# Summing exponentials in pairs on VectorE before the ones-matmul, in the last attention stage of a gated attention block

## The chip, the cores and the metric

One core of a Trainium2 chip runs the whole kernel. The metric is the device time of one execution in microseconds (us), median of three runs. TensorE (PE in the views) does matrix products, VectorE (DVE) and ScalarE (ACT) elementwise work, GpSimd (POOL) elementwise work beside them, SyncE (SP) issues the DMAs.

## What is computed

For each of 8 batches of 512 rows by 512 columns, a cross attention with 16 heads of 32 columns, then a quantised feed-forward layer, both added to the input with a gate:

```python
qk = jnp.einsum('bhqd,bhkd->bhqk', Q, K)
scores = qk / math.sqrt(dk)
# a first softmax gives statistics; a tiny MLP makes one temperature t per head of them
t = jnp.exp(log_t)[..., None]
attn_scores = qk / (2.0 * t)
attn = jax.nn.softmax(attn_scores, axis=-1)
out = jnp.einsum('bhqk,bhkd->bhqd', attn, V)
...
x = x + jnp.tanh(g_xattn[0]) * _L0_xattn_ref(_layernorm(x, axis=-1), ctx_1024, ctx_1024, ...)
x = x + jnp.tanh(g_ffn[0]) * _L0_ffn_ref(_layernorm(x, axis=-1), L0_ffn_w1, L0_ffn_w2)
```

So a score matrix is exponentiated twice: once for the statistics ("first softmax", stage A), once with the temperature ("second softmax", stage B). The change is in stage B of the last batch.

## The kernel before

**Rounds.** A software pipeline of ten rounds, i = -1 to 8. Round i does the projections of batch i+1, stage A of batch i, and stage B with everything behind it of batch i-1. So round 8 has only stage B of batch 7, its output projection, its feed-forward layer and the stores: no stage A and no projections. Each engine has its own instruction list, written out by hand in the order of its work; engines meet only at counting semaphores.

**Stage B.** The 16 heads are taken in four groups G of four heads. For each group the 512 keys are taken in four tiles k of 128. One "set" s = 4G + k (0 to 15) is one key tile of the four heads of a group, that is four score tiles g = 0 to 3 of 128 keys x 512 queries. For each score tile:

- `score_b` (L1519): TensorE makes the tile in one of two PSUM buffers `b_ps`, tile g in buffer g % 2. Before it, it waits until ScalarE has exponentiated the tile two before it, which was in the same buffer.
- `second_exp` (L837): ScalarE writes exp(scale x score) in 32 bits to `probs`, which is the SBUF buffer `region1`, two sets deep. For its first tile of a set it waits until the set that used that half before was consumed (`set_used`).

For each set:

- `values` (L1525): four float32 products (32 output rows each, one per head, side by side in TensorE's columns), exponentials times V, into PSUM `o_ps`, summed over the four key tiles of the group. It waits for all four exponentials of the set.
- `denominators` (L1540): four float32 products of the same shape with a matrix of ones, into PSUM `z_ps`: the sums of the exponentials over the keys. Their end is counted in `set_used`.

TensorE's order in the loop over s is: score tiles 0 and 1 of set s, `values` of set s-1, score tiles 2 and 3 of set s, `denominators` of set s-1. After set 15 come its `values` and `denominators`, and then the output projection (L1596 in round 8).

**Once per group** VectorE normalises (`normalise` L1072) in three parts: part 0 copies `o_ps` out (L1080), during set 4(G+1); part 1 waits for the last `denominators` of the group, transposes `z_ps` (L1083) and makes reciprocals (L1085 to L1087), as the first thing in set 4(G+1)+1; part 2 transposes the reciprocals back (L1090) between tiles 1 and 2 of that set. GpSimd then runs `split_y` (L614): a product (L616), a cast (L618), a subtraction (L620), which give the two float16 halves of y for the output projection. Behind group 0's `split_y`, GpSimd's list has `add_bias` (L576): four additions of a 128x512 tile of the residual and a bias row (L581). All of these GpSimd instructions read and write SBUF. VectorE has no other work in round 8 until the output projection.

`qst` and `kst` hold queries and keys in float16, one of two copies for each batch's parity. Batch 7 uses copy 1; copy 0 was last read in round 7.

The other rounds run the same stage B with the score tiles of stage A put between (`set_tiles`); there VectorE has a maximum and a statistic to do for each of those tiles.

Of the kernel before, what the change touches and what calls it, by code (L numbers as in the profile page):

```python
# [19 lines left out]
F32 = mybir.dt.float32  # L20
F16 = mybir.dt.float16
F8 = mybir.dt.float8e4
ALU = mybir.AluOpType
ACT = mybir.ActivationFunctionType
# [4 lines left out]
H, DK = 16, 32  # L29
HID = 2048  # L30
DH = 64
T = S // P
# [3 lines left out]
G4 = P // DK  # L36
# [8 lines left out]
OFFSET = 1536.0  # L45

SETS = C * T


A_PLAN = (40, (2, 2, 2, 2, 1, 1, 1, 1, 1, 1, 1, 1, 2, 2, 2, 2))  # L50
# [90 lines left out]
def nth(b, per, k):  # L141


    return (b + 1) * per + k
# [23 lines left out]
def stages(i):  # L168

    return 0 <= i < B, 1 <= i <= B, i + 1 < B  # L170


def flamingo_kernel(nc, x, ctxT, g_xattn, g_ffn, WqT, bq, WkT, bk, WvT, bv, WoT, bo,
                    w1T, b1, w2T, b2, w3T, b3, f1T, f2T, out):
    with ExitStack() as ctx:
        def sb(name, shape, dt=F32):
            return ctx.enter_context(nc.sbuf_tensor(name, shape, dt))

        def sem(name):
            return ctx.enter_context(nc.semaphore(name))  # L180
# [4 lines left out]
        qst = [sb(f"qst{p}", [P, H, S], F16) for p in range(2)]  # L185
        kst = [sb(f"kst{p}", [P, H, S], F16) for p in range(2)]
# [6 lines left out]

        region1 = sb("region1", [P, 2, T * S])
        probs = region1[:, :, :].rearrange("p s (g q) -> p s g q", g=G4)
        stage_q = region1[:, 0, :].bitcast(F16).rearrange("p (l g n) -> p l g n", l=2, g=C)
        xin = region1[:, 1, :].rearrange("p (t n) -> p t n", t=T)
        xq = region1[:, 1, :].rearrange("p (t n) -> p t n", t=T)
# [34 lines left out]
        ones32 = sb("ones32", [P, P])  # L233
# [49 lines left out]
        def bank(name):  # L283
            return ctx.enter_context(nc.psum_tensor(name, [P, S], F32))

        a_ps = [bank(f"a_ps{n}") for n in range(A_BANKS)]
        b_ps = [bank(f"b_ps{n}") for n in range(2)]
        o_ps, z_ps = bank("o_ps"), bank("z_ps")
# [27 lines left out]
        def per_batch(name, events):  # L316
            s = sem(name)
            per[name] = (s, events)
            return s
# [6 lines left out]
        b_full = per_batch("b_full", H * T)  # L326
        b_exp = per_batch("b_exp", H * T)
        set_used = per_batch("set_used", SETS)
        o_full = per_batch("o_full", C)
        o_out = per_batch("o_out", C)  # L330
        z_out = per_batch("z_out", C)
# [28 lines left out]
        inv2t_done = per_batch("inv2t_done", 1)  # L360
        f_link = per_batch("f_link", LINKS_F)
        hq_done = per_batch("hq_done", T)

        def slot_of(n):
            return (n % G4) * C + n // G4
# [10 lines left out]
        def set_tiles(i, s):  # L376

            sets = a_plan(i)[0]
            if stages(i)[1]:
                if s == 0:  # L380
                    return {}
                first, end = (EARLY + (sets - EARLY) * n // (SETS - 1) for n in (s - 1, s))
            else:
                first, end = (sets * n // SETS for n in (s, s + 1))
            count = end - first
            return {g: first + n for n, g in enumerate({1: (1,), 2: (0, 2), 3: (0, 1, 2)}[count])}
# [390 lines left out]
        def _(act):  # L777
# [59 lines left out]
            def second_exp(b, s, g):  # L837
                slot = slot_of(G4 * (s // T) + g)
                act.wait_ge(b_full, nth(b, H * T, G4 * s + g + 1))
                if s == 0 and g == 0:  # L840
                    act.wait_ge(inv2t_done, nth(b, 1, 1))
                if g == 0:
                    act.wait_ge(set_used, nth(b, SETS, s - 1))
                nc.scalar.activation(probs[:, (s + 1) % 2, g, :], b_ps[g % 2][:, :], ACT.Exp,  # L844
                                     scale=inv2t[:, slot:slot + 1]).then_inc(b_exp, 1)

            def body(i, par):
                has_a, has_b, has_p = stages(i)
                for s in range(SETS):
                    for g in range(G4):  # L850
# [169 lines left out]
        def _(dve):  # L1020
            vec = nc.vector
# [44 lines left out]
            def tile_a(b, k):  # L1066

                row_max(b, k)
                if k >= S_LATE:
                    row_stat(b, k - S_LATE)  # L1070

            def normalise(b, G, part):  # L1072

                c = Chain(dve, norm_link, LINKS_NORM, b)
                c.n = 3 * G
                z_own = zrow.rearrange("p (j c) -> p j c", c=DK)[:, :, 0]
                if part == 0:
                    dve.wait_ge(o_full, nth(b, C, G + 1))
                    dve.wait_ge(y_done, nth(b, C, G))
                    vec.tensor_scalar(y32, o_ps[:, :], LOWEST, None, ALU.max).then_inc(o_out, 1)  # L1080
                elif part == 1:
                    dve.wait_ge(set_used, nth(b, SETS, T * (G + 1)))
                    vec.transpose(zrow, z_ps[:, :]).then_inc(z_out, 1)  # L1083
                    dve.wait_ge(z_out, nth(b, C, G + 1))
                    c.link(vec.tensor_scalar(zwide[:, :], z_own, 1e-30, None, ALU.max))  # L1085
                    c.link(vec.reciprocal(zwide[:, :], zwide[:, :]))
                    c.link(vec.scalar_tensor_tensor(out=zinv[:, :], in0=z_own, scalar=0.0, in1=zwide[:, :],  # L1087
                                                    op0=ALU.is_ge, op1=ALU.mult))
                else:
                    vec.transpose(zrow, zinv[:, :].unsqueeze(2).broadcast_to([P, S // DK, DK])) \  # L1090
                        .then_inc(zrow_done, 1)

            def features(b, par):

# [113 lines left out]
            def stat_x(b, pair):  # L1208
                tiles = (2 * pair, 2 * pair + 1)
                for n in tiles:  # L1210
                    dve.wait_ge(x_in[n % 2], b * 32 + 16 * (pair + 1) - 32)
                for n in tiles:
                    ins = vec.bn_stats(st6[:, X_ORDER[n], :], cin[:, n % 2, :])
                ins.then_inc(p_link, 1)
                dve.wait_ge(p_link, nth(b, 2, pair + 1))
                for n in tiles:
                    ins = vec.bn_aggr(mv1[:, X_ORDER[n], :], st6[:, X_ORDER[n], :])
                ins.then_inc(mv1_done, 1)
# [71 lines left out]
            def ternary_sum(k):  # L1290
                dve.wait_ge(f_abs, 1 + max(MAGNITUDE_ORDER.index(n) for n in range(4 * k, 4 * k + 4)))
                vec.tensor_reduce(wsum[:, k:k + 1], wabs[:, k, :], AX.X, ALU.add).then_inc(f_sum, 1)
# [53 lines left out]
            def body(i, par):  # L1346
                has_a, has_b, has_p = stages(i)
                second = i == 0
                for s in range(SETS):
                    for g in range(G4):  # L1350
                        if has_a and g in set_tiles(i, s):
                            tile_a(i, set_tiles(i, s)[g])
                        if has_b and (s % T, g) in NORM_AT and s >= T:
                            normalise(i - 1, s // T - 1, NORM_AT.index((s % T, g)))
                    if has_p and has_b and s in X_STATS_AT:
                        stat_x(i + 1, X_STATS_AT.index(s))
                    if second and s == BIAS_AT:
                        join_biases()
                    if second and s in SUMS_AT:
                        ternary_sum(SUMS_AT[s])  # L1360
                    if second and s in SCALES_AT:
                        ternary_scale(SCALES_AT[s])
                    if second and s in TERNARY_AT:
                        make_ternary(TERNARY_AT[s])
# [5 lines left out]
                if has_b:  # L1370
                    normalise(i - 1, C - 1, 0)
                    normalise(i - 1, C - 1, 1)
# [31 lines left out]
                if has_b and has_p:  # L1404
                    c.link(residual_stat(i, T - 1))
                    for t in range(T):
                        ins = vec.bn_aggr(mv2[:, t, :], st6[:, t, :])
# [59 lines left out]
        def _(pe):  # L1467
            mat = nc.tensor.matmul
# [56 lines left out]
            def values(i, has_p, b, par, s):  # L1525

                G, k = s // T, s % T
                pe.wait_ge(b_exp, nth(b, H * T, G4 * (s + 1)))
                if k == 0 and G > 0:
                    pe.wait_ge(o_out, nth(b, C, G))  # L1530
                if s == 0:
                    rested(i, has_p, [o_ps, z_ps])
                for g in range(G4):
                    n = G4 * G + g
                    ins = mat(o_ps[g * DK:(g + 1) * DK, :], vbuf[par][:, k, n * DK:(n + 1) * DK],  # L1535
                              probs[:, (s + 1) % 2, g, :], start=k == 0, stop=k == T - 1)
                if k == T - 1:
                    ins.then_inc(o_full, 1)

            def denominators(b, s):  # L1540

                G, k = s // T, s % T
                if k == 0 and G > 0:
                    pe.wait_ge(z_out, nth(b, C, G))
                for g in range(G4):
                    ins = mat(z_ps[g * DK:(g + 1) * DK, :], ones32[:, 0:DK], probs[:, (s + 1) % 2, g, :],  # L1546
                              start=k == 0, stop=k == T - 1)
                ins.then_inc(set_used, 1)

            def body(i, par):  # L1550
# [283 lines left out]
```

## Time and profile before

| | |
|---|---|
| median of 3 runs | 1297.36 us (1297.17 to 1297.47) |
| the profiled execution | 1297.59 us |
| its span, first to last instruction | 1295.8 us |
| mean granted TensorE clock | 0.970 of full |
| TensorE busy | 1167.2 us (90% of the span) |
| VectorE busy | 1072.5 us (83%) |
| ScalarE busy | 945.0 us (73%) |
| GpSimd busy | 463.5 us (36%) |

Busy shares are of the whole span. Stage B of batch 7 is the stretch from about 1191 to 1239 us of it. Rows of the trace give a start and a duration; "x2" or "x8" is a run of so many instructions in one row, and its duration is that of the run. A matmul row of the float32 products counts two instructions for each of the four tiles, so "x8" is one `values` or one `denominators`. A duration of TensorE contains the time for its result to come out, so that back-to-back instructions overlap: starts, not durations, show its pace.

### The profile page before, as it was taken

Reading aid. Unit: us, or ns where it says so; the run is one execution under the profiler, and the core shown is the slowest. Engines: PE = TensorE matmul, PEld = TensorE weight load, DVE = VectorE, ACT = ScalarE, POOL = GpSimd, SP = SyncE. Lnnn points to the kernel's source line nnn. Section 1 sums busy time; section 2 is a strip of 40 time slices with the busy share of each in tenths; the row PEclk is TensorE's granted clock in tenths of the full one; section 3 lists DMA queues with packets and bytes.
Section 4 is the critical chain, followed back from the end, with each engine's and each line's share of the span. In section 5 each row is a group of like instructions: output and inputs, shape, how many; then the busy total and the mean of one; then the engine's idle time right before and its main releaser. Section 6 shows DMA issues by size and latency. Waiting matters only on the chain.

```text
span 1295.8 us, 19185 instructions
## 1 busy us (share of the span) xinstructions
PE 1167.2 (90%) x6644; PEld 435.0 (34%) x6644; DVE 1072.5 (83%) x1968; ACT 945.0 (73%) x1593; POOL 463.5 (36%) x523
## 2 busy tenths in 40 slices
PE   4867589999999999999999999999999999969978
PEld 2322211444124432344224431344224431224224
DVE  6699779897898889887998879897898879984256
ACT  4588689676985779675985779765985769775833
POOL 3138566520553226530463226511463203120320
PEclk9969789999999999999999999999999999979989
DMA  8822130211202230102202221012202220001000
GB/s 301 233 80 66 37 95 17 50 43 56 66 17 50 58 104 20 42 22 61 90 18 49 50 74 58 21 29 66 98 17 50 50 66 1 1 0 66 1 1 33
DMA packets 36400, 73.09 MB, mean 56 GB/s; under 512 B 8656, under 2 KB 9040, under 8 KB 35792
## 3 DMA queue, kind: packets, MB, share of 16 engines
q1 hardware_dynamic: 36304, 71.87, 19.6%
q8 instruction: 53, 0.87, 0.3%
q14 instruction: 43, 0.35, 0.1%
HBM read 38.13 MB, written 8.39 MB: 36 GB/s over the span
## 4 chain that ended last, share of the span: by engine, by line
PE 50%; DVE 30%; ACT 8%; issue 5%; POOL 1%; SPq 1%; DMA 0%; POOLq 0%; DVEq 0%; ACTq 0%
DVE nmax L1042 8%; DVE stat L1052 6%; PE b_ps L1492 6%; PE b_ps L1522 6%; PE o_ps L1740 6%; PE z_ps L1546 6%; PE o_ps L1535 6%; PE a_ps L1516 4%; PE o_ps L1492 4%; DVE hmax L1254 3%; PE z_ps L1492 2%; PE z_ps L1740 2%; ACT region L844 2%; PE b_ps L1706 2%; ACT etile L812 2%
## 5 line engine op out<-in xcount | busy, mean ns | idle before, releaser
L812 ACT ACTIVATE etile<-a_ps,nmax 128x512 f32<-128x512 f32 x512 | 352.1, 702 | 87.9 <-DVE nmax L1042 86.7
L1042 DVE TENSOR_REDUCE nmax<-a_ps 128x1 f32<-128x512 f32 x512 | 345.4, 679 | 57.5 <-PE a_ps L1516 55.6
L844 ACT ACTIVATE region<-b_ps,inv2t 128x512 f32<-128x512 f32 x512 | 335.0, 704 | 46.8 <-PE b_ps L1522 43.0
L1052 DVE BATCH_NORM_STATS2 stat<-etile 128x6 f32<-128x512 f32 x492 | 335.3, 684 | 10.2 <-ACT etile L812 10.1
L1516 PE MATMUL a_ps<-kst,qst 96*128 96x512 f16 x512 | 196.3, 392 | 31.7 <-ACT etile L812 25.7
L1522 PE MATMUL b_ps<-qst,kst 97*128 97x512 f16 x512 | 193.8, 388 | 11.0 <-ACT region L986 5.6
L1535 PE MATMUL o_ps<-region,vbuf 128*32 128x512 f32 x1024 | 137.2, 607 | 15.0 <-DVE region L1080 8.7
L708 POOL TENSOR_TENSOR region<-region 128x512 f16<-128x512 f32 x64 | 76.6, 1198 | 193.7 <-ACT region L887 193.2
L1546 PE MATMUL z_ps<-region,ones 128*32 128x512 f32 x1024 | 136.4, 604 | 8.1 <-DVE region L1083 8.1
L1522 PEld LDWEIGHTS b_ps<-qst,kst 97*128 97x128 f16 x512 | 49.6, 97 | 251.0 <-ACT region L844 201.9
L616 POOL TENSOR_TENSOR region<-region 128x512 f32<-128x512 f32 x32 | 40.9, 1277 | 245.8 <-DVE region L1090 245.8
L1254 DVE TENSOR_REDUCE hmax<-region 128x1 f32<-128x512 f32 x128 | 81.9, 679 | 17.6 <-ACT region L976 16.0
L586 POOL CAST c_hi<-cin 128x512 f16<-128x512 f32 x28 | 17.1, 611 | 211.3 <-DMA cin<-in_ctxT_dram 211.1
L1516 PEld LDWEIGHTS a_ps<-kst,qst 96*128 96x128 f16 x512 | 51.0, 100 | 86.4 <-ACT etile L812 36.5
L1740 PE MATMUL o_ps<-f,region 128*128 128x512 fp8e4 x352 | 79.6, 379 | 0.0
L1706 PE MATMUL b_ps<-f,region 128*128 128x512 fp8e4 x256 | 63.1, 384 | 5.9 <-DVE region L1280 3.0
L634 POOL TENSOR_SCALAR cin<-cin,mv,rstd 128x512 f32<-128x512 f32 x28 | 58.0, 2081 | 1.5
L976 ACT ACTIVATE region<-b_ps,xmax 128x512 f32<-128x512 f32 x64 | 43.1, 689 | 17.1 <-PE b_ps L1706 16.1
L986 ACT ACTIVATE region<-b_ps 128x1024 f16<-128x1024 f16 x31 | 31.7, 1023 | 30.6 <-PE b_ps L1717 30.5
L1080 DVE TENSOR_SCALAR region<-o_ps 128x512 f32<-128x512 f32 x32 | 21.8, 680 | 36.0 <-PE o_ps L1535 35.8
L1740 PEld LDWEIGHTS o_ps<-f,region 128*128 128x128 f16 x352 | 33.8, 98 | 38.0
L1535 PEld LDWEIGHTS o_ps<-region,vbuf 128*32 128x32 f32 x1024 | 21.0, 108 | 68.2 <-issue 56.9
(325 smaller groups left out, 1997.9 us busy)
## 6 DMA issues: line engine op xcount, KB each, us to landing
kst<-region SPq DMA_DIRECT2D x96, 128.0 KB, 2.3
qst<-region SPq DMA_DIRECT2D x84, 128.0 KB, 2.3
xres<-in_x_dram SPq DMA_DIRECT2D x8, 1024.0 KB, 5.4
out_dram<-xres SPq DMA_DIRECT2D x32, 256.0 KB, 2.0
cin<-in_ctxT_dram SPq DMA_DIRECT2D x30, 256.0 KB, 2.9
cin<-in_x_dram SPq DMA_DIRECT2D x28, 256.0 KB, 2.6
kst<-in_f1T_dram SPq DMA_DIRECT2D x2, 1024.0 KB, 9.8
qst<-in_f2T_dram SPq DMA_DIRECT2D x2, 1024.0 KB, 9.3
```

The costliest lines, as they stand in the source:

```text
L812: nc.scalar.activation(etile[:, k % E_SLOTS, :], a_ps[k % A_BANKS][:, :], ACT.Exp, bias=nmax[:, slot_of(n), t:t + 1], scale=1.0, accum_out ...
L844: nc.scalar.activation(probs[:, (s + 1) % 2, g, :], b_ps[g % 2][:, :], ACT.Exp, scale=inv2t[:, slot:slot + 1]).then_inc(b_exp, 1)
L1042: vec.tensor_reduce(nmax[:, slot_of(k // T), k % T:k % T + 1], a_ps[k % A_BANKS][:, :], AX.X, ALU.max, negate=True).then_inc(a_max, 1)
L1052: vec.bn_stats(stat[:, slot_of(k // T) * T + k % T, :], etile[:, k % E_SLOTS, :]).then_inc(a_stat, covered)
L1254: ins = vec.tensor_reduce(hmax[:, n:n + 1], hbuf[t % 2][:, n * S:(n + 1) * S], AX.X, ALU.max, apply_absolute_value=True)
L1492: ins = mat(mm_ps[bank_n][:, :], left[l](c), right[r](c), start=(c, l, r) == pairs[0], stop=(c, l, r) == pairs[-1])
L1516: mat(a_ps[k % A_BANKS][:, :], qst[par][0:SHIFT, slot, t * P:(t + 1) * P], kst[par][0:SHIFT, slot, :], start=True, stop=True).then_inc(a_f ...
L1522: mat(b_ps[g % 2][:, :], kst[par][0:SHIFT + 1, slot, k * P:(k + 1) * P], qst[par][0:SHIFT + 1, slot, :], start=True, stop=True).then_inc(b ...
L1535: ins = mat(o_ps[g * DK:(g + 1) * DK, :], vbuf[par][:, k, n * DK:(n + 1) * DK], probs[:, (s + 1) % 2, g, :], start=k == 0, stop=k == T - 1)
L1546: ins = mat(z_ps[g * DK:(g + 1) * DK, :], ones32[:, 0:DK], probs[:, (s + 1) % 2, g, :], start=k == 0, stop=k == T - 1)
L1706: ins = mat(mm_ps[bank_n][:, :], xqT[:, c, t * P:(t + 1) * P], f1[:, c, n * S:(n + 1) * S], start=c == 0, stop=c == C - 1)
L1740: ins = mat(mm_ps[bank_n][:, :], hT[t % 2][:, k, :], f2[:, k, :], start=k == 0, stop=k == KC - 1)
```

## The change

In batch 7 alone (`LAST = 7`):

- Two more buffers, each two sets deep, are laid over the free copies: `more_probs` over `kst[0]` for exponentials, `pair_sum` over `qst[0]` for sums. Sets with s % 4 in (0, 1) write to `probs`, those with s % 4 in (2, 3) to `more_probs`.
- `add_pair`: at every odd set s, VectorE adds, tile by tile, the exponentials of set s-1 and set s (float32, 128x512, both from SBUF, the result to SBUF). These 32 additions are in VectorE's list at (s, g), behind the part of `normalise` that stands at that place.
- `denominators` does nothing for even s. For odd s it waits for the four additions and runs its four products on the sums. Eight of the sixteen groups of four products are left.
- ScalarE's wait for a free buffer becomes one wait per two sets, on the pair two before.

```diff
+        more_probs, pair_sum = (a[:, :, :].bitcast(F32).rearrange("p (s g n) q -> p s g (n q)", s=2, g=G4)
+                                for a in (kst[0], qst[0]))
...
+        def exps(b, s):
+            if in_pairs(b) and s % 4 >= 2:
+                return more_probs[:, s % 2, :, :]
+            return probs[:, (s + 1) % 2, :, :]
...
-                if g == 0:
+                if g == 0 and not in_pairs(b):
                     act.wait_ge(set_used, nth(b, SETS, s - 1))
-                nc.scalar.activation(probs[:, (s + 1) % 2, g, :], b_ps[g % 2][:, :], ACT.Exp,
+                elif g == 0 and s % 2 == 0:
+                    act.wait_ge(set_used, nth(b, SETS, max(0, s // 2 - 1)))
+                nc.scalar.activation(exps(b, s)[:, g, :], b_ps[g % 2][:, :], ACT.Exp,
...
-                    dve.wait_ge(set_used, nth(b, SETS, T * (G + 1)))
+                    dve.wait_ge(set_used, nth(b, SETS, T * (G + 1) // (2 if in_pairs(b) else 1)))
...
+            def add_pair(b, s, g):
+
+                j = s // 2
+                dve.wait_ge(b_exp, nth(b, H * T, G4 * s + g + 1))
+                if j >= 2:
+                    dve.wait_ge(set_used, nth(b, SETS, j - 1))
+                vec.tensor_tensor(pair_sum[:, j % 2, g, :], exps(b, s - 1)[:, g, :], exps(b, s)[:, g, :], ALU.add) \
+                    .then_inc(pair_done, 1)
...
+                        if in_pairs(i - 1) and s % 2 == 1:
+                            add_pair(i - 1, s, g)
...
-                              probs[:, (s + 1) % 2, g, :], start=k == 0, stop=k == T - 1)
+                              exps(b, s)[:, g, :], start=k == 0, stop=k == T - 1)
...
                 G, k = s // T, s % T
-                if k == 0 and G > 0:
+                if in_pairs(b) and s % 2 == 0:
+                    return
+                begin = k == (1 if in_pairs(b) else 0)
+                if begin and G > 0:
                     pe.wait_ge(z_out, nth(b, C, G))
+                if in_pairs(b):
+                    pe.wait_ge(pair_done, G4 * (s // 2 + 1))
                 for g in range(G4):
-                    ins = mat(z_ps[g * DK:(g + 1) * DK, :], ones32[:, 0:DK], probs[:, (s + 1) % 2, g, :],
-                              start=k == 0, stop=k == T - 1)
+                    ins = mat(z_ps[g * DK:(g + 1) * DK, :], ones32[:, 0:DK],
+                              pair_sum[:, s // 2 % 2, g, :] if in_pairs(b) else exps(b, s)[:, g, :],
+                              start=begin, stop=k == T - 1)
                 ins.then_inc(set_used, 1)
```

## Rows read from the trace of the kernel before

**Rows 1.** Busy time and clock of a stretch: PE, PEld, DVE, ACT, POOL, PEclk, DMA, GB/s

```profile
1204.00:1216.00 12.00, 12.00 (x81) 2.75 (x80) 2.46 (x7) 10.02 (x16) 8.00 (x7) 1.00 0.01 1
```

**Rows 2.** Chain of work that ended last, inside stage B: start, us, what

```profile
1212.72 0.54 PE b_ps L1522 x2
1213.26 0.99 PE o_ps L1535 x8
```

**Rows 3.** Timeline, a regular half set of stage B

```profile
1194.21 0.60 PE L1522 MATMUL b_ps<-qst,kst 97*128 97x512 f16 x2
1194.64 1.27 ACT L844 ACTIVATE region<-b_ps,inv2t 128x512 f32<-128x512 f32 x2 [0.27 <-PE b_ps L1522]
1194.75 1.06 PE L1535 MATMUL o_ps<-region,vbuf 128*32 128x512 f32 x8
1195.74 0.60 PE L1522 MATMUL b_ps<-qst,kst 97*128 97x512 f16 x2
```

**Rows 4.** Timeline, the half set whose exponentials began late

```profile
1200.82 1.27 ACT L844 ACTIVATE region<-b_ps,inv2t 128x512 f32<-128x512 f32 x2 [0.31 <-PE b_ps L1522]
1201.88 0.65 PE L1522 MATMUL b_ps<-qst,kst 97*128 97x512 f16 x2
1202.14 0.10 PEld L1522 LDWEIGHTS b_ps<-qst,kst 97*128 97x128 f16 x1 [0.17 <-ACT region L844]
```

**Rows 5.** Timeline, the end of stage B

```profile
1236.09 1.27 ACT L844 ACTIVATE region<-b_ps,inv2t 128x512 f32<-128x512 f32 x2 [0.27 <-PE b_ps L1522]
1237.41 1.06 PE L1535 MATMUL o_ps<-region,vbuf 128*32 128x512 f32 x8
1238.29 1.04 PE L1546 MATMUL z_ps<-region,ones 128*32 128x512 f32 x8
```

**Rows 6.** Timeline, set 3's denominators and what follows on VectorE and GpSimd

```profile
1202.46 1.06 PE L1546 MATMUL z_ps<-region,ones 128*32 128x512 f32 x8
1205.06 0.71 DVE L1090 STREAM_TRANSPOSE region<-zinv 128x512 f32<-128x512 f32 x1
1205.42 1.27 ACT L844 ACTIVATE region<-b_ps,inv2t 128x512 f32<-128x512 f32 x2 [0.27 <-PE b_ps L1522]
1205.85 1.28 POOL L616 TENSOR_TENSOR region<-region 128x512 f32<-128x512 f32 x1 [47.69 <-DVE region L1090]
1207.20 0.61 POOL L618 CAST region<-region 128x512 f16<-128x512 f32 x1
1207.89 1.16 POOL L620 TENSOR_TENSOR region<-region 128x512 f16<-128x512 f32 x1
1209.01 4.99 POOL L581 TENSOR_TENSOR xres<-xres,bias_row 128x512 f32<-128x512 f32 x4
1209.59 0.60 PE L1522 MATMUL b_ps<-qst,kst 97*128 97x512 f16 x2
```

**Rows 7.** Timeline, start of the kernel, VectorE and GpSimd alone

```profile
19.49 0.54 DVE L1195 TENSOR_SCALAR region<-region,mv,rstd 128x512 f32<-128x512 f32 x1
19.95 0.68 DVE L1205 TENSOR_TENSOR x_more<-region,x_more 128x512 f16<-128x512 f32 x1
19.97 1.68 POOL L708 TENSOR_TENSOR region<-region 128x512 f16<-128x512 f32 x1 [1.97 <-ACT region L887]
20.55 1.38 DVE L1193 TENSOR_SCALAR region<-region,mv,rstd 128x512 f16<-128x512 f32 x1
24.66 2.25 DVE L1205 TENSOR_TENSOR region<-region 128x512 f16<-128x512 f32 x2
25.09 1.27 POOL L708 TENSOR_TENSOR region<-region 128x512 f16<-128x512 f32 x1 [1.09 <-ACT region L887]
```

**Rows 8.** All instructions of a line: ns min/median/max, first and last start us, form

```profile
L1205 DVE TENSOR_TENSOR region<-region x2: 680/1162/1643, 24.7 to 25.3; 128x512 f16<-128x512 f32 x2
```

**Rows 9.** Stretches of 2 us with TensorE's busy time, granted clock, DMA, GB/s

```profile
1250.00:1252.00 2.00, 0.00 (x0) 1.00 0.00 0
1252.00:1254.00 2.00, 0.00 (x0) 0.80 0.00 0
```

More of the change, by code:

```diff
@@ L47 @@
 SETS = C * T
+LAST = 7
 A_PLAN = (40, (2, 2, 2, 2, 1, 1, 1, 1, 1, 1, 1, 1, 2, 2, 2, 2))
@@ L328, in flamingo_kernel @@
         set_used = per_batch("set_used", SETS)
+        pair_done = sem("pair_done")
         o_full = per_batch("o_full", C)
@@ L362, in flamingo_kernel, with in_pairs @@
         hq_done = per_batch("hq_done", T)
+        def in_pairs(b):
+            return b == LAST
+        def exps(b, s):
+            if in_pairs(b) and s % 4 >= 2:
+                return more_probs[:, s % 2, :, :]
+            return probs[:, (s + 1) % 2, :, :]
         def slot_of(n):
```

## The prediction

> **What bounds the kernel now.** The change touches only stage B of batch 7, so I read that stage alone. First the busy time by stretches: TensorE is busy in all of 12 us, at full clock, ScalarE in 10.0, VectorE in 2.5 and GpSimd in 8.0 [rows 1]. That looks like a stage bound by TensorE. Next the chain of work that ended last: it stays on TensorE here, two score tiles for 0.54 us, four float32 products for 0.99, and again [rows 2]. A half set is thus 1.533 us, a set 3.07, two sets 6.13.
>
> Then the timeline of a half set, to see how near the others are [rows 3]. Score pair at 1194.21; its exponentials start 0.43 later, at 1194.64, and the pair takes 1.27, to 1195.91; the products start at 1194.75; the next score pair at 1195.74. A run of two scores is 0.60 with the second one's own 0.38 in it, so the second score starts about 0.22 behind the first, at 1195.96. That second score has to wait for the second exponential, which ended at 1195.91, 0.05 before. So TensorE is full, but its second score starts at the first moment at which the exponentials allow it. The proof that this is an edge is the one place where the exponentials began late: 0.47 after their scores (1200.35, half a set before 1201.88), they ended at 1202.09, and the second score came at 1202.14, released by ScalarE, instead of 0.22 after 1201.88 [rows 4]. Two loops have the same length here: TensorE's own work, and scores - exponentials - scores through two PSUM buffers.
>
> **The change part by part.**
>
> *The eight groups of ones-products removed.* Each costs TensorE 0.99 us, eight are 8 us, and by busy time alone that would be the gain. What is late next? Take an odd set; its third score starts at time 0, the sums that used to follow its fourth score are gone. Exponentials of tiles 2 and 3: 0.43 to 1.70. Tile 0 of the next set needs the first of them; tile 1 needs the second, so starts at 1.70 + 0.05 = 1.75. The products of `values` start 0.32 behind the second score (1194.75 less 1194.43), at 2.07. With the sums in place it was 0.54 + 0.99 + 0.54 = 2.07. The whole 0.99 becomes a wait for ScalarE's exponentials. From there on the half sets are the old ones: 1.53 each. So seven of the eight removed groups give 0.0 us each, with an uncertainty of about 0.02 each (the 0.43 was 0.47 once), 0.15 together. The eighth is the one of set 14, in set 15: before, `values` of set 15 started at 1237.41, right behind the last exponential (1236.09 + 1.27) [rows 5]; the sums in front were over by then. 0 again. Total gain: 0.0, at most 0.2.
>
> *ScalarE's waits* are on the pair two before, consumed two sets earlier: 0. The exponentials go to another SBUF address: same instruction, 0.
>
> *The 32 additions on VectorE.* The nearest row is a subtraction of two SBUF tiles of that size: 0.68 us alone, the next instruction given 0.60 behind its start [rows 7, 8]. That hides easily in a plain odd set: the exponentials of its tiles end 0.69 or so after they start, the last at 1.70, an addition ends at 2.4, and the sums are wanted on TensorE only behind the second half of the next set, at 0 + 2.07 + 0.99 + 0.54 = 3.60. 1.2 us of cover. At the end, the last addition runs from 1237.4 to about 1238.1, the sums are wanted at 1238.29 [rows 5]: 0, with 0.15 of cover.
>
> *Sets 5, 9 and 13* have `normalise` in front of the additions. Set 3's sums start at 1202.46; VectorE has the reciprocals at 1205.06, where L1090 starts today [rows 6]. Now two additions come first (1205.06, 1205.66), L1090 runs 1206.26 to 1206.97, the third addition starts at 1206.86, the fourth at 1207.46, ending 1208.14. The tiles' exponentials are done by 1206.69, so VectorE is the late one. The sums of set 5 are wanted at 1202.46 + 6.13 = 1208.59. Still 0.4 of cover, if VectorE is not held.
>
> *It will be held, by GpSimd.* L616 starts when L1090 is over, now at about 1207.05: in the middle of the additions. The trace shows what two such instructions do to each other [rows 7]: a VectorE subtraction at 19.95 and a GpSimd subtraction at 19.97; the latter takes 1.68 where L620, of the same form, takes 1.16 [rows 6], so it was held until 20.49, 0.14 before the former's end. VectorE's next instruction, given at 20.55, takes 1.38 instead of 0.54: held until 21.39, 0.26 before GpSimd's end. And of the two subtractions at 24.66, the second took 1.64 instead of 0.68 [rows 8]: held until 26.23, 0.13 before GpSimd's end at 26.36; GpSimd, which had come at 25.09, got in between two VectorE instructions that stood back to back. So: one at a time; whoever waits gets in at the other's next boundary; a VectorE addition holds for 0.54, GpSimd gives back 0.13 to 0.26 before its end, I take 0.20.
>
> Set 5 by these: the third addition holds 1206.86 to 1207.40; L616 runs 1207.40 to 1208.68 and gives back at 1208.48; fourth addition 1208.48 to 1209.16, seen on TensorE 0.05 later, 1209.21. Wanted at 1208.59: 0.62 late. TensorE's list is in order, so the scores of the next set queue behind those sums, and with them the exponentials. Nothing gives this back, because both loops above are full. The same for sets 9 and 13: 3 x 0.62 = 1.9 us.
>
> Set 7 has the bias additions. L618 waits for the fourth addition (holding to 1209.02), 0.61, then L620, 1.16, to 1210.86; the four L581 follow at once, 1.24 apart when alone [rows 6]. Set 7's first scores were at 1209.59, now 1210.21; their exponentials end at 1211.33 and 1211.9, those of tiles 2 and 3 by 1213.5. The first L581 gives back at 1211.90. From there the two engines take turns, 0.54 for an addition and 1.08 for an L581, 1.62 a turn: additions start at 1211.90, 1213.52, 1215.14 and 1216.76, the last ends at 1217.44, seen at 1217.49. Wanted at 1208.59 + 6.13 + 0.62 = 1215.34. 2.15 late. GpSimd is then done; group 1's and group 2's `split_y` end before the next plain set, so sets 11 and 15 are clean.
>
> Sum: 0.0 + 3 x 0.62 + 2.15 = +4.0 us. Bounds: with 0.26 given back, 3 x 0.56 + 1.9 = 3.6; with 0.13, 3 x 0.69 + 2.45 = 4.5; if VectorE cannot get in between the four L581 (no row shows it), its four additions follow at 1215.6 and set 7 is 2.8 late: 4.7. The Trainium skill, page "SBUF — State Buffer", section "SBUF: two separate sides", says that VectorE and GpSimd take turns on a shared pair of ports, each for its full instruction. The trace agrees on the turns, but not on the full duration (given back 0.13 to 0.26 early). By the page the turns would be 0.68 + 1.28, set 5 would be 0.95 late and set 7 3.5: +6.4.
>
> The profiled execution took 1297.59, 0.23 above the median of the runs; 1297.59 + 4.0 - 0.23 = 1301.4.
>
> **The rivals.** 0.2% is 2.6 us here; less than that is no change by this measurement.
> - *Nothing gained, nothing lost* (1297.4, 17%): the additions are hidden after all, because two float32 inputs on VectorE and GpSimd's product do not meet as at 20 us. For it: 0.4 and 1.2 us of cover. Against: rows 7 show the same kinds of instruction. The sums would be released by TensorE's order, not by VectorE.
> - *VectorE keeps its place between back-to-back additions* (1298 to 1299.5, 10%): sets 5, 9 and 13 on time, only set 7 late by up to 2.1. Against: the instruction of 25.09, which got in.
> - *Full turns, as by the page* (1303.8, 8%).
> - *The clock* (1303.4, 9%): in the stall of set 7 TensorE idles some 2 us beside other waits. Elsewhere it idled from 1250 and the clock fell in the second 2 us [rows 9]. If it fell here, about 4 us of work at half clock would add 2. Against: the 2 us before the fall were still at 1.00.
> - *TensorE's time is given back* (1290.4, 6%): seven times 0.99. It needs the second score of a pair at 0.22 behind the first though its buffer's exponential is running. It decides at ScalarE's pair: shorter than 1.27 from score to score. Rows 4 speak against it.
>
> **How the numbers follow.** Forecast as worked out, 50%, with a range of its own from 1300.4 to 1302.3. Slower by over 0.2%: forecast, full turns and clock, 0.67. Within: the first two rivals, 0.27. Faster: 0.06. The range that holds 8 in 10 takes in the first two rivals below and most of the two above: 1297.0 to 1303.5.
>
> **What would show it.** In the profile after: TensorE busy 8 us less; where a group of sums is gone, score pairs 1.2 us and more apart, with waits for L844, and `values` still 2.07 behind the third score; the sums (L1546's successor) waiting for VectorE's additions in sets 5, 7, 9, 13, most in 7; additions of over 1 us beside L616 and L581, and L581 in four rows over 6 us instead of 4.99. The forecast is wrong if additions stay at 0.68 beside GpSimd, or if a score starts before the exponential two before it is over.

## The result, and the profile after

| | before | changed |
|---|---|---|
| median of 6 runs | 1297.36 us | 1302.09 us |
| range | 1296.33 to 1297.58 | 1301.05 to 1302.72 |
| ratio | | 1.0039, 95% interval 1.0028 to 1.0050 |
| profiled execution, span | 1297.59, 1295.8 us | 1301.05, 1299.3 us |
| TensorE, VectorE busy | 1167.2, 1072.5 us | 1162.8, 1098.8 us |

The median became 4.7 us longer, clear of the noise; 4.0 had been forecast. In the changed kernel L1547 makes the scores, L858 the exponentials, L1560 is `values`, L1576 the ones-products, L1113 the additions, L1104 the transpose that ends the normalisation, L628, L630 and L632 `split_y`, L593 the bias additions.

First the places where a group of ones-products is gone. Timeline of the changed kernel, set 5 (start, us, engine, line, what):

```profile
1202.97 0.61 PE L1547 MATMUL b_ps<-qst,kst 97*128 97x512 f16 x2
1204.14 0.39 PE L1547 MATMUL b_ps<-qst,kst 97*128 97x512 f16 x1 [0.57 <-ACT region L858]
1204.71 0.39 PE L1547 MATMUL b_ps<-qst,kst 97*128 97x512 f16 x1 [0.19 <-ACT region L858]
1205.03 1.07 PE L1560 MATMUL o_ps<-region,vbuf 128*32 128x512 f32 x8
```

Where [rows 3] had pairs 1.53 apart with products between them, the next score now comes 1.17 behind the third, its partner 0.57 later, both released by ScalarE, and `values` starts at 2.06: the 2.07 of before. Nothing was gained there.

Then VectorE and GpSimd in the same stretch:

```profile
1203.04 1.29 DVE L1113 TENSOR_TENSOR qst<-region 128x512 f32<-128x512 f32 x2
1204.25 0.70 DVE L1104 STREAM_TRANSPOSE region<-zinv 128x512 f32<-128x512 f32 x1
1204.87 2.33 DVE L1113 TENSOR_TENSOR qst<-region 128x512 f32<-128x512 f32 x2
1205.03 1.63 POOL L628 TENSOR_TENSOR region<-region 128x512 f32<-128x512 f32 x1 [47.30 <-DVE region L1104]
1206.03 0.60 PE L1547 MATMUL b_ps<-qst,kst 97*128 97x512 f16 x2
1207.35 1.06 PE L1576 MATMUL z_ps<-qst,ones 128*32 128x512 f32 x8 [0.71 <-DVE qst L1113]
1208.87 6.30 POOL L593 TENSOR_TENSOR xres<-xres,bias_row 128x512 f32<-128x512 f32 x4
1209.50 6.22 DVE L1113 TENSOR_TENSOR qst<-kst 128x512 f32<-128x512 f32 x4 [2.29 <-ACT kst L858]
1212.95 0.61 PE L1547 MATMUL b_ps<-qst,kst 97*128 97x512 f16 x2
1215.78 1.93 PE L1576 MATMUL z_ps<-qst,ones 128*32 128x512 f32 x8 [2.22 <-DVE qst L1113]
1217.64 1.03 PE L1547 MATMUL b_ps<-qst,kst 97*128 97x512 f16 x2
1217.78 0.72 DVE L1097 STREAM_TRANSPOSE region<-z_ps 128x512 f32<-128x512 f32 x1 [1.46 <-PE z_ps L1576]
1218.60 1.20 PE L1560 MATMUL o_ps<-region,vbuf 128*32 128x512 f32 x8
1219.74 0.60 PE L1547 MATMUL b_ps<-qst,kst 97*128 97x512 f16 x2
1223.57 1.06 PE L1576 MATMUL z_ps<-qst,ones 128*32 128x512 f32 x8 [0.16 <-DVE qst L1113]
```

Two additions alone take 1.29; the two that meet L628 take 2.33, and L628 takes 1.63 instead of the 1.28 of [rows 6]. The four that meet the bias additions take 6.22, and those 6.30 instead of 4.99. The sums of set 5 start at 1207.35; without the wait they would have started 0.53 behind the scores of 1206.03, at 1206.56: 0.79 late. Set 7: 1212.95 + 0.53 = 1213.48, started at 1215.78: 2.30 late. By the same reading sets 5, 7, 9 and 13 are late by 0.79, 2.30, 0.23 and 0.79. (The number in brackets in a row, 0.71 or 2.22, is the idle time that the profile counts; the lateness is 0.07 or 0.08 more.)

The ones-products of set 7 then took 1.93 us instead of 1.06 and the scores behind them 1.03 instead of 0.60. Busy time and clock of that stretch, changed kernel (us, PE, PEld, DVE, ACT, POOL, granted clock, DMA, GB/s):

```profile
1204.00:1216.00 12.00, 7.99 (x48) 1.77 (x52) 9.71 (x9) 8.07 (x14) 9.99 (x7) 0.98 0.00 1
1216.00:1220.00 4.00, 4.00 (x20) 0.45 (x12) 2.41 (x7) 1.27 (x2) 0.00 (x0) 0.63 0.00 0
```

Of these 12 us TensorE was busy in 7.99, against 12.00 [rows 1], and the clock fell to its half level (1.2 GHz) for about 3 us: in stretches of 1 us it is 0.76 from 1215, 0.50 from 1216 and 1217, 0.53 from 1218 and 1.00 from 1219. From the ones-products to the next scores took 1.86 instead of 1.00, from the scores to `values` 0.96 instead of 0.53, from `values` to the scores 1.14 instead of 1.00: 1.4 us in all.

In what follows "the stage" is the time from the first `values` of batch 7 to the first product of the output projection in the profiled execution. It was 47.58 us before (1191.68 to 1239.26) and 53.05 after (1189.70 to 1242.75): +5.5, of which the stalls are 4.1 and the clock 1.4. The rows at its two ends, of the kernel before and then of the changed kernel:

```profile
1191.68 1.07 PE L1535 MATMUL o_ps<-region,vbuf 128*32 128x512 f32 x8 [0.50 <-ACT region L844]
1239.26 0.39 PE L1596 MATMUL b_ps<-wo_hi,region 128*128 128x512 f16 x1
1189.70 1.07 PE L1560 MATMUL o_ps<-region,vbuf 128*32 128x512 f32 x8 [0.50 <-ACT region L858]
1242.75 0.39 PE L1627 MATMUL b_ps<-wo_hi,region 128*128 128x512 f16 x1
```

Behind the stage both kernels take 56.5. The spans differ by 3.5 only, because the code ahead of the stage, the same in both, was 2.0 us shorter in this execution; over the profiles of this study the stage began between 1189.7 and 1193.8. So its length is given below beside the medians of whole runs.

### The profile page after: what moved, and what is told of

It is laid out like the page before. It is cut to its first block, busy times and chain, and to the rows that moved or that the text cites. A ratio compares the mean times of both kernels' runs of the same rounds, so it can differ in the third digit from the quotient of the medians.

```text
span 1299.3 us, 19108 instructions
## 1 busy us (share of the span) xinstructions
PE 1162.8 (89%) x6580; PEld 433.0 (33%) x6580; DVE 1098.8 (85%) x2000; ACT 944.3 (73%) x1593; POOL 466.1 (36%) x523
## 4 chain that ended last, share of the span: by engine, by line
PE 47%; DVE 32%; ACT 8%; issue 6%; POOL 1%; SPq 1%; DMA 0%; POOLq 0%; DVEq 0%; ACTq 0%
DVE nmax L1056 8%; PE b_ps L1517 6%; DVE stat L1066 6%; PE o_ps L1771 6%; PE z_ps L1576 5%; PE b_ps L1547 5%; PE o_ps L1560 5%; PE a_ps L1541 4%; PE o_ps L1517 4%; DVE hmax L1277 3%; PE z_ps L1517 2%; PE z_ps L1771 2%; ACT region L858 2%; PE b_ps L1737 2%; ACT etile L824 2%
## 5 line engine op out<-in xcount | busy, mean ns | idle before, releaser
L858 ACT ACTIVATE region<-b_ps,inv2t 128x512 f32<-128x512 f32 x480 | 314.7, 705 | 46.6 <-PE b_ps L1547 42.7
L1547 PE MATMUL b_ps<-qst,kst 97*128 97x512 f16 x512 | 195.5, 390 | 16.3 <-ACT region L1000 5.6
L1560 PE MATMUL o_ps<-region,vbuf 128*32 128x512 f32 x960 | 128.9, 608 | 14.8 <-DVE region L1094 8.7
L1547 PEld LDWEIGHTS b_ps<-qst,kst 97*128 97x128 f16 x512 | 48.7, 97 | 253.7 <-ACT region L858 190.9
L628 POOL TENSOR_TENSOR region<-region 128x512 f32<-128x512 f32 x32 | 41.8, 1308 | 246.5 <-DVE region L1104 246.5
L1576 PE MATMUL z_ps<-region,ones 128*32 128x512 f32 x896 | 119.4, 605 | 8.1 <-DVE region L1097 8.1
L1517 PE MATMUL b_ps<-region,wq_hi 128*128 128x512 f16 x128 | 41.1, 404 | 3.2 <-ACT region L929 3.2
L636 POOL TENSOR_SCALAR rstd<-mv 128x2 f32<-128x2 f32 (+1 forms) x25 | 5.7, 229 | 105.6 <-DVE mv L1432 44.9
```

Of the source, the lines that this page charges most:

```text
L858: nc.scalar.activation(exps(b, s)[:, g, :], b_ps[g % 2][:, :], ACT.Exp, scale=inv2t[:, slot:slot + 1]).then_inc(b_exp, 1)
L1517: ins = mat(mm_ps[bank_n][:, :], left[l](c), right[r](c), start=(c, l, r) == pairs[0], stop=(c, l, r) == pairs[-1])
L1547: mat(b_ps[g % 2][:, :], kst[par][0:SHIFT + 1, slot, k * P:(k + 1) * P], qst[par][0:SHIFT + 1, slot, :], start=True, stop=True).then_inc(b ...
L1576: ins = mat(z_ps[g * DK:(g + 1) * DK, :], ones32[:, 0:DK], pair_sum[:, s // 2 % 2, g, :] if in_pairs(b) else exps(b, s)[:, g, :], start=be ...
```

## The experiments

Each kernel was timed beside the kernel before, whose median was 1297.17 us beside e1 to e4, 1297.52 beside e5 to e8 and 1297.21 beside e9 to e12. The ratios are to these.

| | median us | ratio | interval | the stage us |
|---|---|---|---|---|
| before | 1297.36 | 1 | | 47.58 |
| changed | 1302.09 | 1.0039 | 1.0028 to 1.0050 | 53.05 |
| e1 half the sums, no additions | 1297.04 | 0.9999 | 0.9990 to 1.0008 | 47.54 |
| e2 bias first | 1302.92 | 1.0042 | 1.0028 to 1.0056 | 52.33 |
| e3 transpose last | 1300.28 | 1.0022 | 1.0013 to 1.0031 | 50.02 |
| e4 both | 1301.70 | 1.0026 | 1.0015 to 1.0037 | 51.88 |
| e5 before, four score buffers | 1296.66 | 0.9992 | 0.9983 to 1.0001 | 47.54 |
| e6 changed, four score buffers | 1302.21 | 1.0035 | 1.0023 to 1.0048 | 52.71 |
| e7 e4 and four buffers | 1296.43 | 0.9989 | 0.9980 to 0.9998 | 46.76 |
| e8 e1 and four buffers | 1294.85 | 0.9977 | 0.9966 to 0.9987 | 45.27 |
| e9 e3, bias gated | 1297.34 | 1.0000 | 0.9991 to 1.0009 | 47.66 |
| e10 e9 and four buffers | 1295.62 | 0.9985 | 0.9976 to 0.9994 | 45.73 |
| e11 e10, products together | 1292.95 | 0.9966 | 0.9952 to 0.9979 | 43.00 |
| e12 before, four buffers, products together | 1292.68 | 0.9961 | 0.9949 to 0.9974 | 43.32 |

### Does the removed work give anything back? (e1)

```diff
-                if in_pairs(b):
-                    pe.wait_ge(pair_done, G4 * (s // 2 + 1))
...
-                              pair_sum[:, s // 2 % 2, g, :] if in_pairs(b) else exps(b, s)[:, g, :],
+                              exps(b, s)[:, g, :],
...
-                        if in_pairs(i - 1) and s % 2 == 1:
-                            add_pair(i - 1, s, g)
```

It also raises batch 7's sums to at least 1e20 instead of 1e-30 ahead of the reciprocal (the clamp, L1099 of the changed kernel); the instruction is the same one with another constant.

> This kernel is the one before with the eight groups of ones-products of the even sets of batch 7 left out and nothing put in their place: no additions on VectorE, no wait for them. It leaves out half of the softmax denominator there (and clamps the rest), so its output is not the reference's. Theory A (the loop scores - exponentials - scores is as long as TensorE's own work): the 8 us of TensorE work turn into waits for ScalarE, time 1297.4 us, within 0.3 of before; two sets stay at 6.13 us. Rival (TensorE is the bound): 7 x 0.99 us come back, 1290.4 us.

Measured: 1297.04 us, ratio 0.9999; the stage 47.54. Timeline of e1, one pair of sets (L1545 scores, L1558 values, L1572 ones-products):

```profile
1210.42 0.60 PE L1545 MATMUL b_ps<-qst,kst 97*128 97x512 f16 x2
1210.85 1.27 ACT L858 ACTIVATE kst<-b_ps,inv2t 128x512 f32<-128x512 f32 x2 [0.27 <-PE b_ps L1545]
1211.59 0.39 PE L1545 MATMUL b_ps<-qst,kst 97*128 97x512 f16 x1 [0.56 <-ACT kst L858]
1212.17 0.39 PE L1545 MATMUL b_ps<-qst,kst 97*128 97x512 f16 x1 [0.19 <-ACT kst L858]
1212.49 1.07 PE L1558 MATMUL o_ps<-kst,vbuf 128*32 128x512 f32 x8
```

Busy times of a stretch of e1:

```profile
1192.00:1204.00 12.00, 10.49 (x68) 2.24 (x64) 1.73 (x4) 9.49 (x16) 0.00 (x0) 1.00 0.30 102
```

Scores at 1210.42, values at 1212.49: 2.07, as with the ones-products between them. TensorE is busy 10.49 of 12 us where it was 12.00, and no faster. So TensorE's work alone is not the bound: without an eighth of its work the stage is as long, and its scores are released by ScalarE. Whether TensorE's own work is shorter than that loop or just as long, e1 can't say; e5 below does.

### Where does the loss come from? (e2, e3, e4, e9)

e2 puts the bias additions ahead of `split_y`, e3 moves the transpose behind the four additions, e4 does both:

```diff
+                if has_b and in_pairs(i - 1):
+                    add_bias(i - 1)
+                    split_y(i - 1, 0)
...
-                        if has_b and (s % T, g) in NORM_AT and s >= T:
+                        if has_b and (s % T, g) in NORM_AT and s >= T and not (in_pairs(i - 1) and (s % T, g) == NORM_AT[2]):
...
                             add_pair(i - 1, s, g)
+                            if (s % T, g) == (1, G4 - 1) and s >= T:
+                                normalise(i - 1, s // T - 1, 2)
```

> The changed kernel with GpSimd's four bias additions (L593 there) ahead of group 0's split_y in round 8. They then run at about 1199 to 1204 us, before set 7's additions, and only meet the first addition of set 5. Theory B (VectorE's additions and GpSimd's SBUF instructions take turns, and TensorE waits for the last addition): set 7's stall of 2.3 us and the clock's fall behind it go, set 5 becomes up to 0.8 us later; 2.4 to 3.2 us above before, 1299.8 to 1300.6 us. Rival (the loss is a cost of the additions or buffers themselves): unchanged, about 1302 us.

Measured: 1302.92 us, the stage +4.75. That is far outside the expected range and near the rival's number, but the profile doesn't show the rival's even cost: the ones-products of three sets wait for VectorE, 1.73 us in set 3 and 0.71 in sets 9 and 13, those of sets 5 and 7 don't, and the clock is at 0.50 for about 3 us behind the first. Why set 3, e4 shows.

> The changed kernel with part 2 of the normalisation (the transpose that releases GpSimd's split_y) behind the fourth addition of sets 5, 9 and 13 instead of between the second and third. Theory B: those additions meet no GpSimd instruction, the three stalls of 0.8 us go; the bias additions still meet set 7, later by about 0.4 us: 2.7 us above before, or 4.1 if the clock falls as in the changed kernel's profile, 1300 to 1301.5 us. Rival (a cost of the additions themselves): unchanged, about 1302 us.

Measured: 1300.28 us, the stage +2.44. The three stalls of sets 5, 9 and 13 are gone, and of the ones-products one group waits for VectorE, that of set 7, with 2.28 us. The clock stayed at 1.00 here.

> The changed kernel with both edits: bias additions first, transpose last. All 32 additions are kept, and so are the eight groups of products on their sums. Theory B: no addition is late for TensorE, 1297.4 us, within 0.5 of before, and by theory A no faster either. Rival 1 (TensorE's removed work comes back once the stalls are gone): 1290 to 1292 us. Rival 2 (a cost of the additions themselves): over 1300 us.

Measured: 1301.70 us, outside what was expected and within the second rival's range. The seven executions spread from 1299.01 to 1302.53, and the profiled one is the longest. Timeline of e4, set 3 (L1116 additions, L1581 ones-products, L1565 values):

```profile
1199.09 5.73 DVE L1116 TENSOR_TENSOR qst<-kst 128x512 f32<-128x512 f32 x4 [3.31 <-ACT kst L861]
1199.46 6.50 POOL L593 TENSOR_TENSOR xres<-xres,bias_row 128x512 f32<-128x512 f32 x4 [40.63 <-DMA xres<-in_x_dram]
1204.87 1.07 PE L1581 MATMUL z_ps<-qst,ones 128*32 128x512 f32 x8 [1.73 <-DVE qst L1116]
1206.46 1.94 PE L1565 MATMUL o_ps<-region,vbuf 128*32 128x512 f32 x8
1213.42 1.06 PE L1581 MATMUL z_ps<-qst,ones 128*32 128x512 f32 x8
```

Busy times of a stretch of e4:

```profile
1208.00:1212.00 4.00, 3.65 (x16) 0.54 (x12) 2.68 (x5) 2.53 (x4) 0.31 (x1) 0.50 0.00 0
```

The bias additions start when the residual's DMA has landed, at 1199.46, and that is 0.37 us into the additions of set 3, which I had taken to be over. The collision was moved, not removed: the ones-products of set 3 wait 1.73 us in e2 and in e4, and in both the clock fell afterwards (granted clock 0.50 in this row). In e4 it stayed down for about 7 us, and set 5's ones-products start 8.55 us behind set 3's (1204.87 to 1213.42) where two sets take 6.13: 2.4 us, which with the 1.8 by which set 3 is late makes 4.2 of the stage's +4.30. e9 puts the bias additions where VectorE is counted to be through:

```diff
+                    pool.wait_ge(pair_done, 2 * G4)
+                    add_bias(i - 1, (0, 1))
+                    split_y(i - 1, 0)
+                    pool.wait_ge(pair_done, 4 * G4)
+                    add_bias(i - 1, (2, 3))
```

> The changed kernel with the transpose last, and GpSimd's four bias additions split so that they fall between VectorE's groups: two once the additions of set 3 are counted, two once those of set 7 are. Bias first had put them on top of set 3's additions. Theory B: no group of additions is late for TensorE, no TensorE wait for VectorE over 0.1 us in the stage, its clock stays full: 1297.4 us, within 0.4 of before, and by theory A not faster. Rival (a loss of the additions that no neighbour explains): over 1299 us.

Measured: 1297.34 us, ratio 1.0000; the stage 47.66, no ones-product waits for VectorE. GpSimd in e9, these at their undisturbed lengths:

```profile
1201.01 2.51 POOL L593 TENSOR_TENSOR xres<-xres,bias_row 128x512 f32<-128x512 f32 x2 [43.17 <-DVE qst L1119]
1207.88 1.28 POOL L628 TENSOR_TENSOR region<-region 128x512 f32<-128x512 f32 x1 [4.36 <-DVE region L1110]
1213.51 2.50 POOL L593 TENSOR_TENSOR xres<-xres,bias_row 128x512 f32<-128x512 f32 x2 [2.43 <-DVE qst L1119]
```

All additions and all products of the changed kernel are there, and the whole loss is gone. It came from the meeting with GpSimd, with the clock's fall behind the stall, and within the interval of 0.1% nothing else was lost or won. One meeting is left and costs nothing: the four additions of set 7 run beside the subtraction of `split_y` and take 3.06 us instead of the 2.50 of set 5's, but still end before TensorE wants the sums.

### What would make the removed work count? (e5 to e8, e10 to e12)

Four score buffers, on the PSUM banks that stage A doesn't use in round 8:

```diff
+        def score_ps(b, s, g):
+            return a_ps[g] if b == 7 and s > 0 else b_ps[g % 2]
...
+                if b == 7 and s == 1 and g == 0:
+                    pe.wait_ge(a_exp, nth(b, H * T, H * T))
+                if b == 7 and s > 0:
+                    pe.wait_ge(b_exp, nth(b, H * T, G4 * s + g - 3))
```

> The kernel before, with the score tiles of sets 1 to 15 of batch 7 in four PSUM buffers (a_ps, free in that round) instead of two; a score waits for the exponential of the tile four before. All ones-products kept. Theory A: TensorE's own work is 6.13 us for two sets with or without the exponentials' wait, so nothing moves: 1297.4 us, within 0.3. Rival (the exponentials' loop is the longer of the two): faster by 1 us or more.

Measured: 1296.66 us, 0.4 below the lower end of what was expected; the ratio is 0.9992 with 1 just inside its interval, and the stage is 47.54 as before. No score has to wait for the exponential two before it any more, and TensorE's own work is 6.13 for two sets too: with e1 this shows two loops of one length.

> The changed kernel with four score buffers. Theory A: the loop through ScalarE is no longer the limit; TensorE's work for two sets is 6.13 - 0.99 - 0.11 = 5.03 us, ScalarE's 8 x 0.585 = 4.7; up to 7.7 us come back, less what the additions are late: they are wanted 1.1 us earlier in every pair, so sets 5, 9 and 13 are late by 1.9 each and set 7 by 3.4 or more, 9 us. Together 1298 to 1301 us, between the two kernels. Rival (buffers do not matter): as the changed kernel, 1302 us.

Measured: 1302.21 us, a little above the expected range; the stage 52.71. Four groups of ones-products wait for VectorE, 0.17 to 2.54 us, and one of them runs for 1.93 us, at the half clock. The number is the rival's, but not its reason: four buffers do give something (e8), and these waits, 4.8 us in all, and the clock cover it. The profiled execution took 1305.42, the longest of the five.

> The changed kernel with four score buffers, bias additions first and the transpose last. Theory A and B together: two sets take about 5.03 us, the additions are late by at most 1 us in sets 5, 9 and 13 in all together 2: 1290 to 1292 us, faster than both kernels. Rival (TensorE's removed work cannot come back because ScalarE or VectorE is the next bound): 1296 to 1298 us.

Measured: 1296.43 us, the stage -0.8: far from the expected 1291 and inside the rival's range. Two groups wait for VectorE, 0.96 us in set 3 and 0.24 in the last; the rest of what is missing is the wait that e8 shows.

> The kernel of half the ones-products and no additions (it leaves out half of the softmax denominator of batch 7 and clamps the rest), with four score buffers. Theory A: with the two-buffer loop gone, the removed products come back: two sets 5.03 us, 1289.7 us (7.7 below before). Rival (another limit, for example the wait of the values' products for all four exponentials): little gain, over 1295 us.

Measured: 1294.85 us, the stage -2.3, not -7.7 as the sum had it; the rival's reason holds. Timeline of e8 (L1553 scores, L1566 values):

```profile
1198.59 1.04 PE L1553 MATMUL a_ps<-qst,kst 97*128 97x512 f16 x4
1199.02 1.26 ACT L861 ACTIVATE kst<-a_ps,inv2t 128x512 f32<-128x512 f32 x2 [0.27 <-PE a_ps L1553]
1200.33 1.07 PE L1566 MATMUL o_ps<-kst,vbuf 128*32 128x512 f32 x8 [0.71 <-ACT kst L861]
```

`values` stands behind the second score of the next set and needs the fourth exponential of its own, which was begun 0.6 us after 1199.02: third score to values is 1.74 instead of 2.07, 7 x 0.33 = 2.3. That wait I had not counted in the sums of e6, e7 and e8, though the rival of e8 names it.

> The same with four score buffers. Half sums with four buffers gave the stage 2.3 us less than before, its profile shows values waiting 0.71 us for the fourth exponential of its set. Additions on time: the same 2.3 us less, 1295.1 us. Rival (additions still late): 1296 to 1297 us.

Measured: 1295.62 us, the stage -1.85: 0.5 above what was expected. One group, the last, waits 0.24 us for VectorE.

For e11 and e12 `values` moves behind the fourth score, in front of the ones-products:

```diff
-                            if s > 0 and g == 1:
+                            if s > 0 and g == (3 if i == 8 else 1):
                                 values(i, has_p, i - 1, 1 - par, s - 1)
```

> The same with values of set s-1 behind the fourth score of set s, next to the sums, instead of behind the second. Then values no longer wait for an exponential that was just begun, and the two kinds of float32 products stand together. TensorE per two sets: 8 scores at 0.215, three groups of products at 0.87, and the changes between them, 4.8 us; ScalarE 8 x 0.585 = 4.7, with some idle at each turn, 5.1. 5 to 7 us below before, 1290.5 to 1292.5 us. Rival (additions are late for sums that are wanted 1.2 us earlier in every pair): 1293 to 1296 us.

Measured: 1292.95 us, the stage -4.6, between the forecast and its rival: four ones-product groups wait for VectorE again, 0.45 to 0.90 us. Timeline of e11, the first scores of two pairs of sets with no such wait between them (L1563 scores):

```profile
1196.99 1.04 PE L1563 MATMUL a_ps<-qst,kst 97*128 97x512 f16 x4
1202.08 1.04 PE L1563 MATMUL a_ps<-qst,kst 97*128 97x512 f16 x4
```

Two sets take 5.09 us here, and 5.35 and 5.24 in the other two pairs without such a wait. Where the additions are late two sets take up to 5.87 (1207.43 to 1213.30).

> The kernel before (all sums, no additions) with four score buffers and values behind the fourth score. TensorE keeps its work and loses one change between float16 and float32 products a set, about 0.25 us of 3.07: 15 x 0.25 = 3.7, 1293.7 us. Rival (the order does nothing, TensorE's products are all): 1297.4 us. What the pair sums then bring is the difference between this and the run before it.

Measured: 1292.68 us, 1.0 below what was expected, ratio 0.9961, the stage 43.32, -4.3. Timeline of e12 (L1530 scores, L1543 values, L1554 ones-products):

```profile
1209.61 1.04 PE L1530 MATMUL a_ps<-qst,kst 97*128 97x512 f16 x4
1210.04 2.42 ACT L847 ACTIVATE region<-a_ps,inv2t 128x512 f32<-128x512 f32 x4 [0.40 <-PE a_ps L1530]
1210.58 1.06 PE L1543 MATMUL o_ps<-region,vbuf 128*32 128x512 f32 x8
1211.46 1.04 PE L1554 MATMUL z_ps<-region,ones 128*32 128x512 f32 x8
1212.43 1.04 PE L1530 MATMUL a_ps<-qst,kst 97*128 97x512 f16 x4
```

A set takes 2.82 us instead of 3.07, with every ones-product kept: `values` takes 0.88 to the next float32 group instead of 0.99 to a score, and one change in front of such a group is saved. Without pair sums and with no additions on VectorE it is as fast as e11, and both are faster than before and than the changed kernel. So with four buffers and in this order the removed products do count, 5.09 to 5.35 instead of 5.64 us for two sets, but e11 loses most of this again in its four waits for VectorE. A kernel that has the order of e11 and additions in time was not run.

## Why the prediction was right

- *The removed ones-products give 0.0.* Right, and shown alone: e1 is at 0.9999 with them gone. The 2.07 from third score to values was measured in the changed kernel (2.06) and in e1 (2.07).
- *Sets 5, 9 and 13, 0.62 each.* Measured 0.79, 0.23 and 0.79, 1.8 in all against 1.9; that the total is so near is in part luck, for two terms were too small and one too large. Of the 0.17 more in set 5, 0.07 is the fourth addition, which ended at 1207.20 (L628 gave back 0.14 before its end, not 0.20), and 0.10 is the step from there to TensorE's start at 1207.35, 0.15 where the sum had 0.05. Set 9's is small because the half clock held TensorE up more than VectorE: behind set 7's ones-products the transpose L1097 started after 2.00 us instead of 1.14 (0.86 later), but the next odd set's sums were wanted after 7.56 instead of 6.13 (1.43 later). The difference of 0.57 is what 0.79 lacks; this is worked out from the one trace, and no run was made for it.
- *Set 7, 2.15.* Measured 2.30, and 2.36 in e3 by the same reading.
- *GpSimd as the cause.* Right: e9 removes the meetings that made TensorE wait, and with them all of the loss. In set 7 a turn took 1.6 us, as forecast. The Trainium skill, page "SBUF — State Buffer", section "SBUF: two separate sides", has each engine keep the shared ports for its whole instruction. By an estimate from that, turns of 0.68 + 1.28, set 5 would have been 0.95 and set 7 3.5 late; the trace has 0.79 and 2.30, so here the ports are given back early.
- *The clock*, given 9% as a rival, came with the forecast in the changed kernel's profile and cost 1.4 us there. That is the term the sum lacked: stalls of 4.1 (4.0 forecast), then the clock. Not in every kernel: e3 had the same stall without it. Whether the clock fell in the other five executions isn't known, so the record doesn't show what the median's +4.7 is made of.
- *TensorE's busy time 8 us less.* It fell by 4.4 only, 4.6 of it less in the stage (47.44 to 42.83). In e1, whose clock stayed full, the stage has 6.3 less: where a group is gone the scores beside it stand alone, and then each one's record also holds the time for its result to come out, 0.39 instead of 0.22. The rest, 1.7, goes with the half clock, at which the same products take longer. The eight groups were gone nonetheless: the stage has 250 matmul records instead of 314.
- The median of 1302.1 is 0.7 above the forecast of 1301.4, inside the range of its own.

## What to carry to other kernels

An engine that is busy in 12.00 of 12 us can still stand in a second loop of just the same length; look at whether its next instruction starts at the first moment that the other engine allows. Then cheaper work gives nothing until the buffers are deeper and the consumer stands later in the list: here four score buffers and another order of the same products brought 4.5 us, and pair sums on top brought nothing measurable, because their additions were late again. Before elementwise work with two SBUF inputs goes to an idle VectorE, lay GpSimd's list beside it, DMA landings included: in e4 the same collision came back four sets earlier, because GpSimd's work then started with a DMA's landing.

## What the runs showed of the hardware that was not expected

- A stall of TensorE of 2.3 us was followed by the half clock in the changed kernel and not in e3 (2.36 late); the wait of 1.73 us was followed by it in e2 and in e4. In the 12 us before it started again TensorE had been busy in 7.77 us in the changed kernel, 8.21 in e3 and 8.77 in e4. The half clock cost 1.4 us where it lasted about 3 us (the changed kernel and e2), and 2.4 in e4, where it lasted about 7.
- VectorE does get in between GpSimd instructions that stand back to back: in set 7 of the changed kernel four additions and four bias additions took turns over 6.2 us, 1.6 us a turn. A GpSimd instruction in such a turn costs VectorE less than its length: the addition behind L628 ran on 0.14 us before L628's end.
- Four float32 products followed by four more take 0.88 us (e12), followed by a float16 score 0.97 to 1.00, and a score in front of them costs 0.32 to their start (1194.43 to 1194.75 in [rows 3]) instead of 0.22.
